# Routed experts in place of dense experts in a fused attention and mixture-of-experts block

## The reference

```
x = x + attention(layernorm(x))       # 16 heads of 16 channels, rotary embedding, biases, output projection
x = x + moe(layernorm(x))
moe(x): xc = bf16(x); nf = bf16(rmsnorm(xc) * norm_weight)
    logits = bf16(nf @ gate.T + gate_bias)            # 8 experts
    the top 2 logits per token; w = softmax of the two
    for each expert: p = nf @ W1.T + b1;  g = min(p[even], 7);  lin = clip(p[odd], -7, 7)
        act = g * sigmoid(1.702 g) * (lin + 1);  y = act @ W2 + b2
    out = xc + bf16(sum of w * y over the two chosen experts)
```

## Time and profile before

| | |
|---|---|
| median of 3 runs | 1222.55 us (1220.27 to 1226.99) |
| the profiled execution | 1218.1 us, span 1216.3 us |
| PE busy | 974.2 us (80%), 5241 instructions |
| DVE busy | 861.2 us (71%) |
| ACT busy | 699.3 us (57%) |
| POOL busy | 400.5 us (33%) |
| mean granted TensorE clock | 0.908 |
| DMA | 92.72 MB, mean 76 GB/s |
| chain that ended last | PE 47%, DVE 28%, issue 12%, ACT 4%, DMA 3% |

### The profile page before, as it was taken

One profiled execution on the slowest core, in us unless ns is written; L12 is line 12 of the kernel. 1 busy time (PEld: TensorE's weight loads), 2 busy tenths in 40 slices (PEclk: granted clock), 3 DMA queues, 4 the chain that ended last, 5 costly groups with the idle time before them and its releaser, 6 DMA issues.

```text
span 1216.3 us, 17776 instructions
## 1 busy us (share of the span) xinstructions
PE 974.2 (80%) x5241; PEld 414.5 (34%) x5313; DVE 861.2 (71%) x1702; ACT 699.3 (57%) x905; POOL 400.5 (33%) x344
## 2 busy tenths in 40 slices
PE   4719897879678997898578898887878999996575
PEld 2402222234232443333233343323333444344243
DVE  5723204768658896786586899586966997898797
ACT  2318895746458574764447675664657776771232
POOL 2413304422244334433135334441321333233243
PEclk9759998989899999988799998998989999997686
DMA  4253342303424241333403334241323442411010
GB/s 148 81 111 59 90 90 63 91 27 79 102 53 105 65 100 58 84 82 76 105 26 84 79 91 101 53 109 44 91 67 77 99 105 58 99 41 39 31 52 31
DMA packets 56443, 92.72 MB, mean 76 GB/s; under 512 B 7162, under 2 KB 41346, under 8 KB 53250
## 3 DMA queue, kind: packets, MB, share of 16 engines
q1 hardware_dynamic: 37892, 66.14, 24.0%
q10 hardware_dynamic: 18432, 25.17, 7.1%
HBM read 74.24 MB, written 17.04 MB: 75 GB/s over the span
## 4 chain that ended last, share of the span: by engine, by line
PE 47%; DVE 28%; issue 12%; ACT 4%; DMA 3%; POOL 2%; SPq 2%; another core or an unknown queue 1%; DVEq 0%; ACTq 0%; POOLq 0%
PE OP L644 12%; PE S L630 11%; PE D L616 7%; DVE th_sb L1052 3%; PE A L599 3%; PE D L543 3%; PE BB L599 3%; DVE act_sb L1057 3%; DVE g_sb L1035 3%; PE D L526 2%; DVE acc L1047 2%; DVE l_sb L1037 2%; ACT probs L761 2%; DMA X<-in_x 2%; DVE xn L895 2%
## 5 line engine op out<-in xcount | busy, mean ns | idle before, releaser
L761 ACT ACTIVATE probs<-S 128x1024 f32<-128x1024 f32 x512 | 511.9, 1022 | 245.9 <-PE S L630 239.5
L630 PE MATMUL S<-Qs,Ks 98*128 98x512 bf16 x1024 | 311.9, 397 | 66.1 <-issue 28.5
L644 PE MATMUL OP<-probs,V 128*17 128x512 f32 x2048 | 280.6, 621 | 2.7 <-ACT O L770 2.7
L848 POOL TENSOR_TENSOR act_lo<-act_sb,act_hi 128x512 fp32r<-128x512 f32 x128 | 165.0, 1289 | 224.9 <-DVE act_hi L1063 164.6
L616 PE MATMUL D<-W,act_hi 128*128 128x256 f32 x448 | 138.3, 338 | 40.9 <-DVE Vn L935 20.0
L630 PEld LDWEIGHTS S<-Qs,Ks 98*128 98x128 bf16 x1024 | 80.2, 100 | 252.9 <-issue 95.6
L1047 DVE SCALAR_TENSOR_TENSOR acc<-D,combh,acc 128x256 f32<-128x256 f32 x224 | 97.3, 476 | 79.7 <-PE D L616 79.6
L616 PE MATMUL D<-W,act_lo 128*128 128x256 f32 x448 | 119.0, 295 | 0.0
L842 POOL TENSOR_SCALAR W<-W2b 128x512 fp32r<-128x512 bf16 x64 | 44.2, 690 | 225.7 <-PE D L616 220.8
L737 ACT ACTIVATE th_sb<-g_sb 128x512 f32<-128x512 f32 x128 | 80.1, 626 | 64.0 <-DVE g_sb L1035 63.2
L1052 DVE SCALAR_TENSOR_TENSOR th_sb<-th_sb,g_sb 128x512 f32<-128x512 f32 x128 | 116.3, 909 | 0.1
(11 more groups left out here) (138 smaller groups left out, 1063.4 us busy)
## 6 DMA issues: line engine op xcount, KB each, us to landing
W<-in_w ACTq DMA_DIRECT2D x64, 256.0 KB, 2.7
Ks<-k_scr SPq DMA_DIRECT2D x32, 384.0 KB
W2b<-in_w ACTq DMA_DIRECT2D x64, 128.0 KB, 2.7
Ks<-k_scr SPq DMA_DIRECT2D x32, 256.0 KB
q_scr<-parts SPq DMA_DIRECT2D x16, 384.0 KB, 2.8
k_scr<-parts SPq DMA_DIRECT2D x16, 384.0 KB, 2.5
Qs<-q_scr SPq DMA_DIRECT2D x32, 192.0 KB
X<-in_x SPq DMA_DIRECT2D x8, 512.0 KB, 7.6
```

The source lines that it names most:

```text
L630: last = mm(S[:, j2, C * i:C * (i + 1)], Ks[0:SROWS + MROWS, g % 2, j, P * kt:P * (kt + 1)], Qs[0:SROWS + MROWS, g % 2, j, :], start=True, ...
L644: last = mm(OP[32 * j:32 * j + VW, :], V[:, kt, HG * g + j, :], probs[:, s % 2, C * j:C * (j + 1)], start=kt == 0, stop=kt == KT - 1)
L761: nc.scalar.activation(probs[:, s % 2, 2 * C * j2:2 * C * (j2 + 1)], S[:, j2, :], ACT.Exp, scale=SCALE).then_inc(exp_done, 1)
L848: tt(act_lo[:, e % 2, it, :], act_sb[:, a % 2, :], act_hi[:, e % 2, it, :].bitcast(FP32), ALU.subtract).then_inc(lo_s, 1)
```

## The change

The experts are routed. Only the (token, expert) pairs that were chosen are computed: 1024 rows a unit, sorted by expert, each expert's rows padded to tiles of 128. That is at most NT = 15 tiles, worked on as NPAIR = 8 pairs (the last has one tile), one pair every 3 steps (PACE 6 halves) from half 46.

- "rank" counts with products against a triangular matrix and ones how many earlier rows went to each expert; `place_slots` on DVE (15 linked small operations) makes from it each row's slot (`pos`) and each tile's expert number (`eid`).
- "scatter": POOL writes the rows of nf to their slots in DRAM (`xs`) with indirect DMAs, 8 a unit (2 for each of 4 token tiles, halves 33 to 36).
- SP loads the rows of a pair ("xg", 6 halves ahead, 4 buffers), W1 of its tiles ("w1l", 8 halves ahead) and W2 ("w2l", 2 halves ahead). W1 and W2 are chosen by an expert number that SP reads from SBUF with `value_load`, 30 a unit. W2 comes already widened (256 KB) from a DRAM copy `w2f` that is made once at the start; POOL's "w2" and ACT's `load_expert` are gone.
- "gx": PE transposes the rows (4 transposes), DVE copies them to xgT. "up": 8 products of 128 columns a tile, both halves into the two-bank tile U. DVE adds the biases as tensors (bT, made by a product "bias") for gate and linear, then clips the linear part on both sides. The gate's clip is folded into "hidden" (SWISH_LIMIT).
- "down" is 8 products as before, into D; DVE copies them to ysb, and SP stores them to DRAM (`ys`), 256 KB a pair.
- "gather": POOL fetches each token's two result rows (8 indirect DMAs, halves 98, 99, 102, 103, which are 34, 35, 38, 39 of a later unit), and DVE combines them into acc (8 instructions, halves 101, 102, 105, 106). "final" is at half 107 (it was at 84).

```diff
-    FFN0, LAG, PAIRED = 26, 4, True
-    DOWN, TANH, HIDDEN, UP, LO, W2AT = 0, 2, 2, 1, 5, 3
+    SCATTER = 33
+    FFN0, PACE = 46, 6
+    W1L, XG, W2L, UP, TANH, HIDDEN, LO, DOWN, STORE = -8, -6, -2, 2, 3, 4, 5, 8, 9
...
+    for t in range(TC):
+        place(POST, SCATTER + t, ("scatter", t))
+    for m in range(NPAIR):
+        h = FFN0 + PACE * m
+        for st, off in (("w1l", W1L), ("xg", XG), ("w2l", W2L), ("gx", 0), ("up", UP), ("tanh", TANH), ("hidden", HIDDEN), ("lo", LO),
+                        ("down", DOWN), ("store", STORE)):
+            place(EXPERTS, h + off, (st, m))
+    h = FFN0 + PACE * (NPAIR - 1) + DOWN
+    for a in range(2):
+        place(EXPERTS, h - 4 + 2 * a, ("b2", a))
+    for t in range(TC):
+        place(EXPERTS, h + 2 + t // 2 * 4 + t % 2, ("gather", t))
+        place(EXPERTS, h + 5 + t // 2 * 4 + t % 2, ("combine", t))
+    place(EXPERTS, h + 11, ("final", 0))
...
+    ORDER = ("gx", "up", "down", "tanh", "hidden", "lo", "store", "w2l", "w1l", "xg", "b2", "gather", "combine", "final")
...
@@ SP
+                elif st in ("w1l", "w2l"):
+                    if st == "w1l":
+                        wait_apart(sp, (gating, GATING * u + TILED))
+                        if looped(u) or u or a >= 2:
+                            wait_apart(sp, (m1_mm, NPAIR * u + a - 1))
...
+                    for q in range(tiles_of(a)):
+                        t, to = 2 * a + q, 2 * (a % 2) + q
+                        e = sp.value_load(eid[0:1, n, t:t + 1], min_val=0, max_val=NE - 1)
+                        if st == "w1l":
+                            sp.dma_start(W1[:, to, :, :], w1[bass.ds(e, 1)].rearrange("o p c n -> (o p) c n")).then_inc(w1_ld[a % 2], 16)
+                        else:
+                            sp.dma_start(W2[:, to, :].bitcast(FP32), w2f[bass.ds(e, 1)].rearrange("o p n -> (o p) n")).then_inc(w2_in[a % 2], 16)
+                elif st == "xg":
+                    wait_apart(sp, (sc_s, 16 * TOPK * TC * (u + 1)))
...
+                    sp.dma_start(xg[:, a % 4, 0:nt, :], xs[n][2 * P * a:2 * P * a + P * nt, :].rearrange("(q p) c -> p q c", p=P)
+                                 ).then_inc(xg_ld[a % 4], 16)
+                elif st == "store":
+                    sp.wait_ge(y_s, NPAIR * u + a + 1)
...
@@ PE
+            def expert_up(m, u):
+                i = NPAIR * u + m
+                pe.wait_ge(xgT_s, i + 1)
+                pe.wait_ge(w1_ld[m % 2], weights_in(u, m))
...
+                for q in range(tiles_of(m)):
+                    for k in range(BLOCKS):
+                        cols = slice(P * k, P * (k + 1))
+                        for c in range(CT):
+                            r = P * (CT * q + c)
+                            last = mm(bank[:, q, cols], W1[:, 2 * (m % 2) + q, c, cols], xgT[:, m % 2, r:r + P],
+                                      start=c == 0, stop=c == CT - 1)
...
@@ POOL
-                elif st == "w2":
...
+                elif st == "scatter":
+                    if a == 0:
+                        wait_apart(pool, (gating, GATING * u + PLACED), (nf_s, TC * (u + 1)))
...
+                    for k in range(TOPK):
+                        i = TC * k + a
+                        nc.gpsimd.indirect_dma_start(xs[n], bass.IndirectOffsetOnAxis(ap=pos[:, n, i:i + 1], axis=0),
+                                                     nf[:, a, :], None).then_inc(sc_s, 16)
+                elif st == "gather":
+                    if a == 0:
+                        wait_apart(pool, *((y_w[i], rows_in(u, NPAIR - 1)) for i in range(2)))
+                    if a >= 2:
+                        wait_apart(pool, (comb2_s, TOPK * (TC * u + a - 1)))
...
@@ DVE
+                    for gl, to, done in ((0, g_sb, g_s), (1, l_sb, lb_s)):
...
+                        v.tensor_tensor(to[:, q, 0:w].rearrange("p (q k t) -> p q k t", q=nt, k=2),
+                                        bank[:, 0:nt, FI * gl:FI * (gl + 1)].rearrange("p q (k t) -> p q k t", k=2),
+                                        bT[:, 2 * gl:2 * gl + 2, 2 * m:2 * m + nt].rearrange("p k q -> p q k")[:, :, :, None]
+                                        .to_broadcast([P, nt, 2, P]), ALU.add).then_inc(done, 1)
+                    dve.wait_ge(lb_s, i + 1)
+                    v.tensor_scalar(l_sb[:, q, 0:w], l_sb[:, q, 0:w], 1.0 - LIMIT, 1.0 + LIMIT, ALU.max, ALU.min).then_inc(l_s, 1)
+                if st == "down":
+                    dve.wait_ge(m2_mm, i + 1)
...
+                    v.tensor_copy(ysb[:, q, 0:w], output[:, 0:w]).then_inc(y_s, 1)
```

More of the change, by code:

```diff
@@ L559, in stage @@
                     last.then_inc(d_full, 1)
+                elif st == "rank":
+                    pe.wait_ge(gating, GATING * u + GATES1)
+                    each, width = sel[:, :, :].rearrange("p t e -> p (t e)"), TC * NE
+                    mm(bank[:, 0:width], tri[:, :], each, start=True, stop=False)
+                    for d in range(1, TC):
+                        mm(bank[:, NE * d:width], ones[:, :], each[:, 0:width - NE * d], start=False, stop=d == TC - 1)
+                    for t in range(TC):
+                        last = mm(bank[:, width:width + NE], ones[:, :], each[:, NE * t:NE * (t + 1)], start=t == 0, stop=t == TC - 1)
+                    last.then_inc(d_full, 1)
+                elif st == "bias":
+                    pe.wait_ge(gating, GATING * u + TILED)
+                    for k in range(BLOCKS):
+                        last = mm(bank[:, 2 * NPAIR * k:2 * NPAIR * (k + 1)], b1_sb[:, P * k:P * (k + 1)], oneh[:, :], start=True, stop=True)
+                    last.then_inc(d_full, 1)
                 elif st == "combT":
-                    pe.wait_ge(comb_s, 3 * (u + 1))
+                    pe.wait_ge(comb_s, u + 1)
                     for t in range(TC):
@@ L570, in stage @@
                     last.then_inc(d_full, 1)
+                elif st == "gx":
+                    pe.wait_ge(xg_ld[a % 4], 16 * (NPAIR // 4 * u + a // 4 + 1))
+                    for q in range(tiles_of(a)):
+                        for c in range(CT):
+                            i = CT * q + c
+                            last = nc.tensor.transpose(bank[:, :].bitcast(BF16)[:, P * i:P * (i + 1)], xg[:, a % 4, q, P * c:P * (c + 1)],
+                                                       identb[:, :])
+                    last.then_inc(d_full, 1)
                 elif st == "up":
@@ new lines, in place_slots @@
+                for i in range(3):
+                    link(v.tensor_tensor(ends[i + 1][:, NE:2 * NE], ends[i][:, NE:2 * NE], ends[i][:, NE - 2 ** i:2 * NE - 2 ** i], ALU.add))
+                end = ends[3]
+                link(v.scalar_tensor_tensor(slot[:, :, :], end[:, None, NE - 1:2 * NE - 1].to_broadcast([P, TC, NE]), float(P), before,
+                                            ALU.mult, ALU.add))
+                link(v.tensor_tensor(slot2[:, :, :, :], slot[:, None, :, :].to_broadcast([P, TOPK, TC, NE]), chosen[:, :, :, :], ALU.mult))
@@ new lines, in combine @@
+            def combine(t, u, n):
+                if t == 0:
+                    dve.wait_ge(acc_s, 2 * (u + 1))
+                dve.wait_ge(yg_ld[t % 2], 16 * TOPK * (TC // 2 * u + t // 2 + 1))
+                for k in range(TOPK):
+                    done = TOPK * (TC * u + t) + k
+                    if k:
+                        dve.wait_ge(comb2_s, done)
+                    v.scalar_tensor_tensor(acc[:, t, :], yg[:, t % 2, k, :], wsel[:, n, k, t:t + 1], acc[:, t, :],
+                                           ALU.mult, ALU.add).then_inc(comb2_s, 1)
```

374 lines of the change are left out of this document (222 added, 152 removed), and 2 rows, old and new, of the table AT.

## The result

The kernel after takes 1386.53 us (median of 4 runs, 1382.14 to 1394.15), the kernel before, on the same chip, 1221.41: a ratio of 1.135, 95% interval [1.128, 1.142]. The change costs 165 us; a gain of 45 was forecast. The profiled execution has a span of 1388.8 us (before: 1216.3), and it agrees with the median within 0.3%.

What follows compares the result with a forecast made beforehand. Bounds: TensorE throughput in u7, waits between ordered engines in u2 to u5, VectorE and latency at the end. Terms: u1 -16, u2 to u5 -50, u6 and u7 -14, end +30, start +5; total -45, 1177 us, range 1085 to 1260.

Steps and rivals of the forecast that it cites:

- the middle units: u2 to u5: per unit TensorE -9, shorter waits -10, POOL +4, plus 5 in u3 and u5; together -50 us.
- TensorE, the price of a pair: Per unit: 2.63 us a full pair, "up" products 0.083 each; 20.7 replaces 29.4, saving 9 us.
- VectorE, 24 us less a unit: Per unit: expert work falls from 73 to 49 us; shorter waits taken as 10 a unit in u2 to u5.
- Nothing in mid-kernel.: SP's queue: 39 us of issues and reads a unit, of some 130, cost nothing in mid-kernel.
- cost 0 taken: DMA traffic: some 8.5 MB more a unit, share about doubling to 0.6, at no cost.
- POOL's indirect DMAs: Scatters and gathers at 1.2 us each delay the third combine: +4 a unit in u2 to u7, +5 in u3 and u5.
- rival (b): Third combines and end: everyone waits for POOL, deciding from 1.64 us per indirect DMA; 1312 us at 2.5; chance 0.20.
- u1: Unit u1: 13 half-experts (24 us) become 3 pairs (8), -16 us.
- The end: After the last attention: 150 us against 119.8, +30, with pairs at 6.5 us each.
- rival (d): At the end SP needs 11.3 us a pair against VectorE's 6.5: +36, 1213 us, hardly a change; chance 0.05.
- Rival (c): VectorE holds POOL up: each indirect DMA waits out a 0.45 us cast, +47, 1224 us, no change; chance 0.07.

Runs made afterwards that it cites:

- e14: Routed kernel with a pair every 2 steps, rows loaded 10 halves ahead, combines later, x requested at step 20 of the unit before for both chunks: 1271.9 us.
- e13: e11 with the transposes of the rows put back: 1248.5 us, ratio 1.027.
- e11: Routed kernel with a pair every 2 steps, no weight loads after two pairs, no row transposes, combines later, x early for one chunk: 1198.4 us.
- e10: Routed kernel with x for each batch's second chunk requested at step 20 of the unit before: 1350.3 us.
- e1: Routed kernel with rows of pairs 2 to 7 loaded 12 halves ahead instead of 6: 1365.2 us.
- e15: Kernel before (dense experts) with x requested at step 20 of the unit before, for both chunks: 1211.5 us, ratio 0.996.
- e9: Kernel before with its dense experts 12 halves later (FFN0 38 for 26) and combh doubled, no routing: 1260.8 us, ratio 1.033.
- e6: Routed kernel with a pair every 2 steps instead of 3 (PACE 4), the stages of a pair moved to fit: 1312.3 us.
- e3: Routed kernel with all weight loads and reads kept, but 128 bytes a partition instead of 2048 after the first two pairs: 1370.9 us.
- e2: Routed kernel without weight loads and expert-number reads after the first two pairs: 1322.4 us.
- e4: Routed kernel with combines 6 halves behind their gathers instead of 3, the second two gathers 8 halves behind the first two: 1350.3 us.
- e12: Routed kernel with a pair every 2 steps, pairs from half 42 instead of 46, x early as e10: 1321.4 us.

## Why the prediction was wrong

The step that failed is the middle units: "u2 to u5: 4 x (-9 - 10 + 4) + 2 x 5 = -50", measured +103.5. It took saved busy time of TensorE and VectorE as saved time, and it had no term for the move of the expert work into the next unit's first 16 steps, nor for SP where a unit begins.

A ladder of runs takes the loss apart, each rung one group of edits. After 1386.5; timing alone, nothing left out (e14) 1271.9, -115; no weight loads (e13) 1248.5, -23; no transposes (e11) 1198.4, -50. The second rung isn't pure: e13 has x early for one chunk only and its rows later than e14. If these two help there as they did in e10 and e1, the loads cost more than 23. Against 1218, then: the routed work without its transposes and loads, and well timed, is 20 us faster than the dense one (5 of them the early x would give to that one too, by e15); transposes eat 50; loads 23 or more; and the written order of the change 115.

Step by step:

- **TensorE, the price of a pair: right; what it saves: wrong.** The "up" products took 0.083 us each (75.0 / 904), the value taken. What was not asked is how often TensorE would stand, and at what clock it would then work. The saved 9 us a unit (72 in all) are 10 in its busy time, since the attention products took 55 more at the lower clock, and none in the time.
- **VectorE, 24 us less a unit: right in size (23.6), wrong in worth.** "Where engines wait for each other it shortens waits. ... I take 10 a unit." On the whole they grew: ACT's wait for scores rose from 239.5 to 309.0. In an order where VectorE stands before a transfer, less work ahead of the transfer makes the wait longer (1.64 to 14.70).
- **The step that was missing: the move itself.** The experts start at half 46 in place of 26, so 5 of 8 pairs, with three fillings of D or U each, come to steps 0 to 15 beside the projections. The working had no term for it. e9 shows 42 us for 12 halves, with dense experts, some 25 of it in u2 to u5; e6, which moves the pairs back out of these steps, gains 74. A row for it was to be had: in the kernel before, steps 8 to 15 of u3 take 28.0 us at clock 1.00, and only the last two "down" and the first two "up" lie in them.
- **SP: "Nothing in mid-kernel."** The sum of SP's issue time was not far off (5.0 us for four loads, 4.2 forecast), and its mean is far below the unit. But SP's list is in order too: where a unit begins the loads, the stack and x come in one run, and x, which is wanted next, leaves 7 us late. e3 against e2 prices SP's reads and issues at 48 us, and e10 the x part at 36 (they overlap).
- **DMA traffic: "cost 0 taken".** It was 16 us (e3), of a DMA share that went from 0.34 to 0.48 in u2 and from 0.37 to 0.57 in u6.
- **POOL's indirect DMAs: 1.28 us apart (0.97 to 1.01 and 0.30) for 1.2.** The waits before the combines were longer than costed (14.1 us in u3 where 12 stood; 119.8 over the kernel where 7 a unit and 12 in u3 and u5 make some 50). Their price came out as costed, +34 forecast (4 x 6 + 5 x 2) and 36 by e4, and that is partly luck: twice the wait, and less than half of it on the path. The DMAs stay below rival (b)'s 1.64 us, and they are not what everyone waits for.
- **u1: right** (115 against 116.2): u0's pairs begin only at half 46 of it, so no pair lies in its steps 0 to 15. It is the unit that the move spares.
- **The end: +50 in place of +30.** The last scatter is over at 1295.71, 76 us in, where 71 was costed with its landing. From there to the first of the last gathers (1369.33) it is 74 us where 60 stood (71 to 131). The remaining 19.5 us are as forecast (19). TensorE's order of time, and SP's:

```profile
1299.52 0.58 PE L670 MATMUL D<-identb,xg 128*128 128x128 bf16 x4 [17.18 <-DMA xg<-xs]
1306.72 1.89 PE L699 MATMUL U<-xgT,W 128*128 128x128 bf16 x16 [6.62 <-DVE xgT L1096]
1315.11 0.58 PE L670 MATMUL D<-identb,xg 128*128 128x128 bf16 x4 [6.50 <-DMA xg<-xs]
```

```profile
1306.36 0.40 SPq L522 DMA_DIRECT2D out<-acc  x1
...
1312.28 0.38 SPq L513 DMA_DIRECT2D xg<-xs  x1
...
1317.43 0.38 SPq L513 DMA_DIRECT2D xg<-xs  x1
1320.63 0.38 SPq L518 DMA_DIRECT2D ys<-ysb  x1
...
1325.82 0.38 SPq L513 DMA_DIRECT2D xg<-xs  x1
```

  The rows of the first pair are waited for 17.18 us. Their copy to xgT then stood behind combines of u6 that waited for their gathers (VectorE stood until 1300.18 and came to the copy at 1306.24), 6.62 us. The rows of the second pair stood in SP's list behind the store of u6's output (1306.36) and four weight loads, and its transposes come 15.6 us after the first pair's (1299.52 to 1315.11), where the forecast had 6.5 a pair. From there to the eighth (1355.85) a pair takes 6.8 us on average, so the forecast's 6.5 was near, and rival (d)'s 11.3 was not. The longer of them go by SP's list: of the 8.4 us from 1317.43 to 1325.82, 2.8 are a wait for the data of the store (1317.81 to 1320.63). e11, without the loads, ends in 147.6. The clock is 0.59 there, 0.72 before.
- **Rival (c)** is not supported: the 128 indirect DMAs of the kernel after took 0.94 to 1.31 us each, 115 of them 1.02 or less, so none waited out a cast of 0.45 within its own span. The Trainium skill, "SBUF — State Buffer", "SBUF: two separate sides", says that a DMA issued from GpSimd can't write its descriptors while VectorE runs a two-port operation; these rows show at most 0.37 us of such a hold (1.31 against 0.94).

What stays open: what of the loss the lower clock is; why the first groups of u2 and u4, which hold the turn, are 55 to 63 and 59 to 70 us in the routed runs whatever was eased, against 55.6 and 50.0 before; whether e12 loses by its scatters; and the stores, which make SP wait 271 us in all for VectorE's copies. To move them to another queue was not tried.

## What to carry to other kernels

In a kernel whose engines follow one written order, price a change by what each list waits for at each place and not by its saved busy time: an operation that is taken away may have been the cover of a transfer. Where a change moves work, cost the move by itself: ask what the stretch that receives it looks like now (here clock 1.00, TensorE busy 24.2 of 28.0 us) and how many round trips through a shared bank it gets. Saved work of TensorE can also be lost again to a lower granted clock (here 55 of the 72 us forecast). And a queue whose mean load is low can still be late where its issues bunch, so put the transfer that is wanted first ahead of those that are wanted in eight steps.
